# Two-layer graph attention: the last layer norm of each row block is spread over the next sweep and given to GpSimd, and the last sweep is closed by halves

## The reference, cut to what matters

```python
def _L1_gnn_ref(x, W, a, adj_matrix):          # x: 4096 x 256, W: 4 heads x 256 x 64
    xt = jnp.einsum('ni,hio->hno', x, W)
    src = jnp.einsum('hnf,hf->hn', xt, a[:, :out_f])
    dst = jnp.einsum('hnf,hf->hn', xt, a[:, out_f:])
    e = jax.nn.leaky_relu(src[:, :, None] + dst[:, None, :], NEG_SLOPE)
    e = jnp.where((adj_matrix > 0)[None, :, :], e, -jnp.inf)
    attention = jax.nn.softmax(e, axis=2)
    h_prime = jnp.einsum('hij,hjf->hif', attention, xt)
    return h_prime.transpose(1, 0, 2).reshape(n, heads * out_f)

def _layernorm(x, axis=-1, eps=1e-5):
    m = jnp.mean(x, axis=axis, keepdims=True)
    v = jnp.var(x, axis=axis, keepdims=True)
    return (x - m) / jnp.sqrt(v + eps)

x = _layernorm(x + _L0_gnn_ref(x, adj, ...))   # layer 0, 8 heads of 128
x = _layernorm(x + _L1_gnn_ref(x, W, a, adj))  # layer 1, the part looked at here
```

## Time and profile before

| | |
|---|---|
| median of 3 runs | 2784.57 us |
| the profiled execution, own time | 2785.78 us |
| its span | 2783.4 us |
| PE busy | 2680.3 us (96%) |
| DVE busy | 1988.7 us (71%) |
| ACT busy | 2064.6 us (74%) |
| POOL busy | 570.7 us (21%) |
| granted TensorE clock | 0.993 |

### The profile page before, as it was taken

One profiled execution on the slowest core, in us unless ns is written; L12 is line 12 of the kernel. 1 busy time (PEld: TensorE's weight loads), 2 busy tenths in 40 slices (PEclk: granted clock), 3 DMA queues, 4 the chain that ended last, 5 costly groups with the idle time before them and its releaser, 6 DMA issues. The chain is left out here.

```text
span 2783.4 us, 62400 instructions
## 1 busy us (share of the span) xinstructions
PE 2680.3 (96%) x26475; PEld 2323.0 (83%) x26475; DVE 1988.7 (71%) x3200; ACT 2064.6 (74%) x3216; POOL 570.7 (21%) x453
## 2 busy tenths in 40 slices
PE   7889999999999999999999999999999979999997
PEld 3438887888888888888888888888888879999997
DVE  5465679677676776767777676675655779988897
ACT  4447886777777777777777778777754569999996
POOL 0030018232231422323322232230002320000000
PEclk9999999999999999999999999999999999999999
DMA  7985431010110111111111111011115555323330
GB/s 258 395 322 182 141 116 48 22 36 21 42 30 27 37 27 32 33 31 30 34 30 30 26 33 34 26 39 39 38 58 177 189 192 185 114 79 122 103 109 17
DMA packets 193945, 243.70 MB, mean 88 GB/s; under 512 B 14202, under 2 KB 113786, under 8 KB 193660
## 3 DMA queue, kind: packets, MB, share of 16 engines
q1 hardware_dynamic: 193668, 239.72, 26.8%
HBM read 180.49 MB, written 59.18 MB: 86 GB/s over the span
## 5 line engine op out<-in xcount | busy, mean ns | idle before, releaser
L708 PE MATMUL l_ps<-l_arena 128*128 128x258 f16 x16384 | 1835.1, 273 | 8.0 <-DVE l_arena L1214 3.9
L708 PEld LDWEIGHTS l_ps<-l_arena 128*128 128x128 fp8e4 x16384 | 1592.1, 97 | 248.7 <-DVE l_arena L1214 5.5
L923 ACT ACTIVATE l_arena<-l_arena 128x512 fp8e4<-128x512 f32 x2048 | 1281.4, 708 | 89.2 <-PE l_ps L708 89.1
L1213 DVE SCALAR_TENSOR_TENSOR l_arena<-l_arena,l_mask 128x512 uint32<-128x512 uint32 x512 | 469.0, 916 | 405.7 <-ACT l_arena L923 403.0
L817 PE MATMUL l_ps<-l_arena 128*128 128x130 f16 x8192 | 487.8, 221 | 30.0 <-DVE l_arena L1393 15.6
L817 PEld LDWEIGHTS l_ps<-l_arena 128*128 128x128 fp8e4 x8192 | 483.0, 98 | 34.7 <-DVE l_arena L1393 24.7
L1214 DVE TENSOR_TENSOR l_arena<-l_arena,l_mask 128x512 uint32<-128x512 uint32 x512 | 489.9, 957 | 0.0
L1007 ACT ACTIVATE l_arena<-l_arena 128x1024 fp8e4<-128x1024 f32 x432 | 454.7, 1140 | 5.7 <-PE l_ps L817 5.7
L360 POOL TENSOR_TENSOR l_arena<-l_arena 128x516 f32<-128x516 f32 x120 | 156.7, 1306 | 1263.1 <-PE l_ps L708 1171.7
L941 ACT COPY l_arena<-l_ps 128x258 f32<-128x258 f32 x256 | 93.5, 368 | 245.3 <-PE l_ps L708 245.3
L1219 DVE SCALAR_TENSOR_TENSOR l_arena<-l_ps,l_arena 128x258 f32<-128x258 f32 x256 | 117.0, 481 | 147.9 <-ACT l_arena L941 147.9
(11 more groups left out here) (150 smaller groups left out, 1220.6 us busy)
## 6 DMA issues: line engine op xcount, KB each, us to landing
l_arena<-in_adj SPq DMA_DIRECT2D x128, 512.0 KB, 6.9
l_arena<-uv SPq DMA_DIRECT2D x128, 260.0 KB, 5.5
l_wh<-l_arena SPq DMA_DIRECT2D x64, 256.0 KB, 9.3
l_arena<-l_srow SPq DMA_DIRECT2D x64, 256.0 KB, 3.3
l_arena<-l_wh SPq DMA_DIRECT2D x64, 256.0 KB, 4.7
feat<-l_arena SPq DMA_DIRECT2D x64, 256.0 KB, 2.2
l_arena<-feat SPq DMA_DIRECT2D x32, 512.0 KB, 3.7
uv<-l_arena SPq DMA_DIRECT2D x8, 1040.0 KB, 5.2
```

The costliest lines, as they stand in the source:

```text
L708: last = nc.tensor.matmul(sums(t, m), pattern(k, m).bitcast(F8)[:, j, t * P:(t + 1) * P], uv[:, slot(h, order[k]) + j, 2 * m * W1:2 * (m + ...
L923: ins = act.activation(pattern(k, 0).bitcast(F8)[:, j, :], s1b[q][:, :], ACT.Relu, bias=kc[:, h, jt:jt + 1], scale=STEEP, saturate=False)
L1213: dve.scalar_tensor_tensor(c, v, ONE8X4, m, ALU.bitwise_xor, ALU.bitwise_and)
```

## The change

There are four parts.

- **Statistics in two lots.** In g = 4, 8, 12 VectorE takes the statistics of four tiles behind the split of piece 2 and of four behind that of piece 3; only then come the aggregation and the sum with epsilon. The root on ScalarE stands behind the compares of piece 6 (it stood behind those of piece 3), the reciprocal behind the split of piece 6 (it stood behind that of piece 4).
- **Scaling on GpSimd.** The eight instructions `(z - mean) * rstd` of those sweeps leave VectorE. GpSimd, which has no other work in layer 1, does them as eight `tensor_scalar` of 128x256 with two operands per partition, and signals after four and after eight.
- **Halves.** SyncE stores `z` in two halves of 512 KB as they are signalled, then waits for each store and loads that half of the next block. The addition in `divide2` waits for both loads.
- **The last sweep.** In sweep 15 TensorE takes pieces 6 and 7 together and tile by tile: all matmuls of row tile 0, then of tile 1, and so on. VectorE evacuates, divides and takes the statistics of the first four tiles ahead of the second four; ScalarE scales the first four tiles and two of the others, VectorE the last two; three stores follow, of 512, 256 and 256 KB.

The rest (one semaphore fewer for GpSimd's `scale2`, two unused names) moves nothing.

The core of the diff:

```diff
+            for b in range(NB2 - 1):
+                pool.wait_ge(s_rs2, b + 1)
+                for p in range(2):
+                    for u in range(p * HALF, (p + 1) * HALF):
+                        last = nc.gpsimd.tensor_scalar(z[:, u, :], z[:, u, :], mv[:, u, 0:1], rs[:, u:u + 1],
+                                                       ALU.subtract, ALU.mult)
+                    last.then_inc(s_ap, 1)
...
                 if g > 0 and g % H2 == 0:
-                    sp.wait_ge(s_ap, 2 * (g // H2))
-                    sp.dma_start(tiles(out, g // H2 - 1), z[:, :, :]).then_inc(s_o, 16)
-                    sp.wait_ge(s_o, 16 * (g // H2))
-                    sp.dma_start(z[:, :, :], tiles(x1, g // H2)).then_inc(s_zl, 16)
+                    b = g // H2 - 1
+                    for p in range(2):
+                        sp.wait_ge(s_ap, 2 * b + p + 1)
+                        sp.dma_start(tiles(out, b, p * HALF, (p + 1) * HALF), z[:, p * HALF:(p + 1) * HALF, :]
+                                     ).then_inc(s_o[p], 16)
+                    for p in range(2):
+                        sp.wait_ge(s_o[p], 16 * (b + 1))
+                        load_z(b + 1, p)
...
-                for k in range(CPB):
+                for k in range(CPB - 2 if g == G2 - 1 else CPB):
...
+                if g == G2 - 1:
+                    pe.wait_ge(s_bc2, CPB * G2)
...
+                    for t in range(TPB2):
+                        for k in range(CPB - 2, CPB):
+                            for j in range(JC2):
...
+                        if t < TPB2 - 1:
+                            last.then_inc(s_mm2, 1)
+                    last.then_inc(s_pe2, 2)
...
-                    if g > 0 and g % H2 == 0 and k == ahead2 + 1:
+                    if g > 0 and g % H2 == 0 and k == CPB - 2:
                         final_root(g // H2 - 1)
...
-                        if m == 0:
-                            final_stats(g // H2 - 1, range(TPB2))
-                            final_norm(g // H2 - 1)
-                        if m == 2:
-                            final_scale(g // H2 - 1)
-                        if m in (3, 4):
-                            final_apply(g // H2 - 1, range(4 * (m - 3), 4 * (m - 2)), s_ap)
+                        b = g // H2 - 1
+                        if m < 2:
+                            final_stats(b, range(HALF * m, HALF * (m + 1)), g)
+                        if m == 1:
+                            final_norm(range(TPB2), 2 * NT + 3 * b + 2)
+                        if m == 4:
+                            final_scale(range(TPB2), b + 1)
...
-            final_stats(NB2 - 1, range(TPB2))
-            final_norm(NB2 - 1)
-            final_scale(NB2 - 1)
...
-            final_apply(NB2 - 1, range(TPB2 // 2), s_fin[0])
+            evacuate2(G2 - 1, halves[0])
+            divide2(G2 - 1, 0, HALF, 3 * (G2 - 1))
+            final_stats(NB2 - 1, halves[0], G2)
+            final_norm(halves[0], base + 1)
+            evacuate2(G2 - 1, halves[1])
+            final_scale(halves[0], NB2)
+            last_shift(0)
+            divide2(G2 - 1, HALF, TPB2, 3 * G2)
+            final_stats(NB2 - 1, halves[1], G2 + 1)
+            final_norm(halves[1], base + 4)
+            final_scale(halves[1], NB2 + 1)
+            last_shift(1)
+            for u in range(HALF, HALF + 2):
+                last = dve.tensor_scalar(z[:, u, :], z[:, u, :], mv[:, u, 0:1], rs[:, u:u + 1], ALU.subtract, ALU.mult)
+            last.then_inc(s_fin[1], 1)
```

More of the change, by code:

```diff
@@ L202, in network @@
         CW2 = blk2 // 4
+        HALF = TPB2 // 2
         G2, FIRST = H2 * NB2, H2
@@ L630, in _ @@
                         load_uv(g + 2, k)
-            for p in range(2):
+            for p, (first, last) in enumerate(((0, HALF), (HALF, HALF + 2), (HALF + 2, TPB2))):
                 sp.wait_ge(s_fin[p], 1)
-                sp.dma_start(tiles(out, NB2 - 1)[:, p * TPB2 // 2:(p + 1) * TPB2 // 2, :],
-                             z[:, p * TPB2 // 2:(p + 1) * TPB2 // 2, :]).then_inc(s_o, 16)
-            sp.wait_ge(s_o, 16 * (NB2 + 1))
+                sp.dma_start(tiles(out, NB2 - 1, first, last), z[:, first:last, :]).then_inc(s_o[p % 2], 16)
+            sp.wait_ge(s_o[0], 16 * (NB2 + 1))
+            sp.wait_ge(s_o[1], 16 * NB2)
         @block.tensor
@@ L825, in sweep2 @@
                     last.then_inc(s_pe2, 1)
+                if g == G2 - 1:
+                    pe.wait_ge(s_bc2, CPB * G2)
+                    for k in range(CPB - 2, CPB):
+                        pe.wait_ge(s_uv2[q][k], 16 * (g // 2 + 1))
+                    for t in range(TPB2):
+                        for k in range(CPB - 2, CPB):
+                            for j in range(JC2):
+                                jt = order[k] * JC2 + j
+                                for m in range(2):
+                                    at = jt * W4 + m * 2 * V1
+                                    last = nc.tensor.matmul(sums2(t, m),
+                                                            pattern2(k, m).bitcast(F8)[:, j, t * P:(t + 1) * P],
+                                                            uv2[:, q, at:at + 2 * V1], start=False,
+                                                            stop=(k == CPB - 1 and j == JC2 - 1 and m == 1),
+                                                            skip_group_check=True)
+                        if t < TPB2 - 1:
+                            last.then_inc(s_mm2, 1)
+                    last.then_inc(s_pe2, 2)
             pe.wait_ge(s_id, 4)
@@ L1023, in final_root, with last_root, last_apply @@
                 act.activation(rt[:, :], rt[:, :], ACT.Sqrt).then_inc(s_sq, 1)
+            def last_root(p):
+                half = slice(p * HALF, (p + 1) * HALF)
+                act.wait_ge(s_sd, NB2 + p)
+                act.activation(rt[:, half], rt[:, half], ACT.Sqrt).then_inc(s_sq, 1)
+            def last_apply(p, tiles, signal):
+                act.wait_ge(s_n, 2 * NT + 3 * (NB2 + p))
+                for u in tiles:
+                    ins = act.activation(z[:, u, :], z[:, u, :], ACT.Identity, bias=mv[:, u, 1:2], scale=rs[:, u:u + 1])
+                ins.then_inc(signal, 1)
             for n in range(16):
@@ L1111, in _ @@
                 copy_sums2(g, batch)
[L1112 to L1116 removed]
+            last_root(0)
+            last_apply(0, range(HALF), s_fin[0])
+            last_root(1)
+            last_apply(1, range(HALF + 2, TPB2), s_fin[2])
         @block.vector
@@ L1393, in split2, with evacuate2 @@
                 dve.tensor_tensor(v, v, m, ALU.bitwise_and).then_inc(s_bc2, 1)
-            def evacuate2(g):
-                for t in range(TPB2):
+            def evacuate2(g, tiles):
+                for t in tiles:
                     if g == 0 and t == 0:
@@ L1403, in evacuate2, with divide2, final_stats @@
                                              e2[:, t, :], ALU.mult, ALU.add).then_inc(s_ev2, 1)
-            def divide2(g):
+            def divide2(g, first, last, base):
                 h, b = g % H2, g // H2
-                dve.wait_ge(s_ev2, TPB2 * (g + 1))
-                ch = Chain(dve, s_dv2, 3 * g)
-                ch.link(dve.tensor_tensor(vt2, vt2, e2[:, :, V1:2 * V1], ALU.add))
-                ch.link(dve.reciprocal(zr2[:, :], vt2[:, :, D2:V1].rearrange("p t a -> p (t a)")))
-                v = vt2[:, :, 0:D2]
-                ch.link(dve.tensor_tensor(v, v, zr2[:, :].unsqueeze(2).to_broadcast([P, TPB2, D2]), ALU.mult))
-                if h == 0:
-                    dve.wait_ge(s_zl, 16 * (b + 1))
-                part = z[:, :, h * D2:(h + 1) * D2]
-                dve.tensor_tensor(part, part, v, ALU.add).then_inc(s_dz, 1)
-            def final_stats(b, tiles):
-                dve.wait_ge(s_dz, H2 * (b + 1))
+                dve.wait_ge(s_ev2, TPB2 * g + last)
+                ch = Chain(dve, s_dv2, base)
+                part = vt2[:, first:last, :]
+                inverse = zr2[:, first:last]
+                ch.link(dve.tensor_tensor(part, part, e2[:, first:last, V1:2 * V1], ALU.add))
+                ch.link(dve.reciprocal(inverse, part[:, :, D2:V1].rearrange("p t a -> p (t a)")))
+                v = part[:, :, 0:D2]
+                ch.link(dve.tensor_tensor(v, v, inverse.unsqueeze(2).to_broadcast([P, last - first, D2]), ALU.mult))
+                if h == 0:
+                    dve.wait_ge(s_zl, 32 * (b + 1))
+                into = z[:, first:last, h * D2:(h + 1) * D2]
+                dve.tensor_tensor(into, into, v, ALU.add).then_inc(s_dz, 1)
+            def final_stats(b, tiles, ready):
+                dve.wait_ge(s_dz, ready)
                 for u in tiles:
```

71 lines of the change are left out of this document (35 added, 36 removed).

## The result

| | before | changed |
|---|---|---|
| median, 6 runs each | 2784.82 us | 2809.05 us |
| range | 2783.91 to 2788.46 | 2807.52 to 2812.72 |
| span of the profiled execution | 2783.4 us | 2811.0 us |

The ratio is 1.0087, 95% interval 1.0076 to 1.0097: 24.2 us slower. The forecast was 2784.3 in a range of 2776.5 to 2793, that is, no change that could be told, so it was wrong; slower had a chance of 0.26.

The account below looks back on a forecast made before the run. TensorE, busy 96% of the span, was taken as the bound, with only its gaps and the end to win. Three blocks at +2.7 and the last sweep at -3.0 gave -0.3 us: 2784.3 us, range 2776.5 to 2793.

Parts of the forecast that it names:

- Part 1: Norms inside layer 1: two statistics lots and the later root leave about 1.2 us of each norm's 4.2 us loss.
- Part 4: Last sweep: pieces 6 and 7 tile by tile and closing by halves save 3.0 us, between 2.1 and 3.5.
- h: Time one GpSimd scaling holds VectorE up, taken as 0.3 us; three blocks change by 3 x (8h - 1.5).
- Part 2: Scaling on GpSimd: eight alternate with 7.5 us of VectorE work from 2664.8, ending at 2674.7; VectorE up to 2.1 us later.
- Part 3: Half transfers: second half stored by 2678.1, loaded by 2681.8; VectorE's addition waits 3.9 us, all passed to TensorE.
- rival 2: GpSimd's scaling leaves VectorE alone: eight take 3.6 us, `z` is there at 2675.5, total 2772.6; chance 7%.
- the line through the casts: GpSimd one-input casts, 0.253 us at 16 columns and 0.289 at 128, extended to 0.33 at 256: h = 0.1.
- The high end: GpSimd's scaling as dear as a two-input instruction of 256 columns, 0.724 us: h = 0.6.
- the prediction's own rule: From layer 0's overlapping GpSimd and VectorE instructions: h is the GpSimd instruction's length less 0.2 us.
- about -2 us: The forecast's sum if GpSimd's scaling costs the Trainium skill's estimate of 0.22 us for 256 columns.
- Rival 1: GpSimd's scaling is dear, h above 0.55: over 5.6 us slower, 2791.5 at 0.6 and 2796 at 0.8; chance 26%.

Follow-up runs that it names:

- e6: Changed kernel with a product of two SBUF inputs (`z` times `z`) in place of each GpSimd scaling; 2798.11 us, one run.
- e8: Changed kernel with the root behind the compares of piece 5 and the reciprocal behind the split of piece 5, both 6 before; 2810.32 us, 1.0083.
- e9: Changed kernel whose GpSimd scaling keeps the mean per partition but takes a constant for the root; 2808.98 us, one run.
- e12: Changed kernel with root and reciprocal both behind piece 7 instead of piece 6, so GpSimd starts later; 2809.95 us, 1.0088.
- e5: Changed kernel with two constants instead of the two operands per partition in GpSimd's scalings; 2798.54 us, one run.
- e2: Changed kernel with a second buffer for `z` for odd blocks, next block loaded beforehand, scaling still on GpSimd; 2772.21 us, 0.9955 against the kernel before.
- e1: Changed kernel with the eight scalings of sweeps 4, 8, 12 back on VectorE; 2779.82 us, 0.998 against the kernel before.

## Why the prediction was wrong

The path was right (GpSimd's end, store, load, addition, TensorE), and Parts 1 and 4 held. What failed is the size h of Part 2; a smaller part came from the load of a half in Part 3, and the clock behind a gap had no term. The last norm inside the layer, step by step. Times after are put on the clock of before by taking off 21.94 us (2672.04 - 2650.10, both the start of piece 2 of sweep 12).

| step | predicted | measured |
|---|---|---|
| gaps before pieces 3 and 4 (Part 1) | 0.4, 0.75 | 0.33, 0.56 |
| root's wait (Part 1) | none | none |
| reciprocal issued (Part 2) | 2664.8 | 2664.5 |
| eight scalings end (Part 2) | 2674.7 | 2679.7 |
| last scaling to `z` loaded (Part 3) | 7.1 | 8.2 |
| VectorE is ready to add (Part 3) | 2677.9 | 2678.4 |
| its wait (Part 3) | 3.9 | 9.5 |
| 512 matmuls behind the gap longer (no term) | 0 | 2.55 |
| last matmul to end (Part 4) | 11.8 | 11.3 |

**Part 1 held.** The root now starts behind a compare without a wait, where it stood idle 4.86 us:

```profile
2675.77 5.30 ACT L1043 ACTIVATE l_arena<-l_arena 128x1024 fp8e4<-128x1024 f32 x5
2680.97 0.20 ACT L1059 ACTIVATE l_arena<-l_arena 128x8 f32<-128x8 f32 x1
```

**Part 2 failed**, in the step "GpSimd's eight alternate with them: the last ends at 2664.8 + 7.5 + 8h = 2674.7". Two things in it were wrong. The size: the instruction takes 1.21 us without splits beside it, not 0.45 (rival 2) or 0.5 (h = 0.3 and the 0.2); the upper bound, 0.724 for a two-input instruction of the same size, was no bound at all, since the operation with two constants takes 1.06 and a plain product in e6 0.61. One input is not the cheap case here: the line through the casts did not hold for this operation. The high end was mis-stepped too: 0.724 less 0.2 is 0.52, not 0.6. And the form of the sharing: I took from layer 0's pairs that the engines take turns, so that h comes back on VectorE. That is so for two-input instructions (e6). With an operand per partition VectorE keeps its 1.22, and GpSimd waits, mostly for its pauses (e8, e9, e12). VectorE lost 0.5 us, GpSimd's end 5.0.

Of the two, the size made the loss. By the prediction's own rule 1.21 us give h = 1.0, and the last scaling would end at 2664.8 + 7.5 + 8.1 = 2680.4, 0.7 past the measured 2679.7. Three norms at that h cost 3 x (8.1 - 1.5) = 19.8, and with Part 4 that is 2784.6 + 19.8 - 3.0 = 2801.4; three times the 1.1 of the load and the 6.9 of the clock (both below) make it 2811.6, against 2809.05 measured. The same working for e6 (h = 0.41, 6.0 us behind its gaps) gives 11.6 us over the kernel before, where its one run has 10.8. That the wrong form of sharing came so near in GpSimd's end is luck: in e8 and e12 the start moved and the end hardly did, which no rule of taking turns gives.

A row of the kernel before already pointed at the other form. Rival 2 used the cast L381 that took 1.25 us instead of 0.25, but not what ran beside it, a split instruction that kept its 1.21:

```profile
2267.98 1.25 POOL L381 CAST l_arena<-l_arena 128x16 f16<-128x16 f32 x1
```

```profile
2267.91 1.21 DVE L1392 SCALAR_TENSOR_TENSOR l_arena<-l_arena,l_mask 128x1024 uint32<-128x1024 uint32 x1
```

In that pair GpSimd alone was held up.

The Trainium skill's rule ("SBUF — State Buffer", Who interferes with whom), that such a pair excludes each other for a whole instruction, agrees with e6 (1.63 for a split's instruction, 1.59 for GpSimd's). The same section of the Trainium skill says "Issue order, not op shape, decides who blocks." That does not agree with the runs: e5, e6 and e9 start GpSimd's work at the same place in the code and differ in the instruction alone, and who is held up changes; and in e8 seven instructions of VectorE that started later were done before the one of 9.00 us. The measurement decides.

The estimate of 0.22 us from the Trainium skill, "GPSIMD Engine Reference", 3.1, is off by a factor of 5 against 1.06 to 1.21. The prediction's "about -2 us" by it took h = 0.22; by its own rule, length less 0.2, h is 0.02 and the sum -7.0.

**Part 3** took that end over, one to one as it says: 5.0 more from the scaling, 1.1 more from the transfers, 0.5 less since VectorE was itself that late, 3.9 + 5.0 + 1.1 - 0.5 = 9.5. The halves on the queue and the half transfers:

```profile
2696.84 5.20 SPq L632 DMA_DIRECT2D out<-l_arena  x2
2702.08 3.15 SPq L501 DMA_DIRECT2D l_arena<-x  x2
```

```profile
out<-l_arena SPq DMA_DIRECT2D x2, 512.0 KB, 3.1
l_arena<-x SPq DMA_DIRECT2D x2, 512.0 KB, 4.8
```

The store of a half takes 3.1 to 3.2, about as forecast (3.3). The load was to take 3.7, since I took off it what the store saves; it takes 4.8. It is issued at 2704.86, 2.8 us behind the first, with row and values for later sweeps 0.5 and 1.0 behind it, and the DMA engines are over 90% busy until it lands. How much of the 1.1 each of these costs was not separated:

```profile
2703.40:2705.00 1.60, 0.07 (x2) 0.00 (x0) 0.00 (x0) 1.60 (x3) 0.00 (x0) 1.00 0.99 211
2705.00:2707.00 2.00, 0.00 (x0) 0.00 (x0) 0.00 (x0) 2.00 (x3) 0.00 (x0) 0.60 0.93 269
2707.00:2709.70 2.70, 0.00 (x0) 0.00 (x0) 0.00 (x0) 2.70 (x3) 0.00 (x0) 0.50 0.93 313
```

(Windows: start:end, length, busy time of PE, PEld, DVE, ACT and POOL, granted clock, DMA share, GB/s.)

**A term was missing.** TensorE's granted clock falls in the gap (1.00, 0.60, 0.50 in the windows above) and is low behind it. More windows, same columns:

```profile
2713.50:2716.50 3.00, 3.00 (x29) 3.00 (x30) 3.00 (x4) 0.00 (x0) 0.00 (x0) 0.50 0.84 324
2716.50:2719.50 3.00, 3.00 (x34) 3.00 (x33) 2.12 (x2) 0.00 (x0) 0.00 (x0) 0.57 0.04 12
2719.50:2722.50 3.00, 3.00 (x55) 3.00 (x53) 2.52 (x3) 2.52 (x3) 0.00 (x0) 1.00 0.00 0
```

At 0.50, that is 1.2 GHz, 29 matmuls start in 3 us; at 1.00, in the last window, 55. This costs 2.54, 1.79 and 2.55 us behind the three gaps, 6.9 in sum, over a quarter of the loss of 24.2.

For this norm: 1.2 + 9.5 + 2.55 = 13.3, against 13.45 from the stretch (105.10 less three sweeps of 30.55) and 5.1 as forecast.

**Part 4 held**: 3.5 against 3.0, and no gap before the last 128 matmuls. From the last matmul to the last scaling it is 8.4 us where it was 10.7, and from there to the end 2.9 where it was 4.1.

**The rivals.** Rival 1 named the right place and sign, "an instruction of 0.75 us or more", at 26%. Its price was too low: it stopped at h = 0.8 (2796), where 1.0 was due, and it had neither the slower load nor the clock. Rival 2's premise, VectorE left alone, came nearly true (0.5 us), but its conclusion was the opposite of what happened. I took it that if VectorE is not held, GpSimd isn't either. Who is not held and who is was one question in the forecast, and it is two.

## What to carry to other kernels

A step moved to an idle engine is free only while nobody waits for its end. Follow its end through every buffer back to the bounding engine before moving it, and give it a second buffer first: e2 turned a loss of 24 us into a gain of 12 without making GpSimd a bit quicker. Where no row shows an instruction in its very form, a row of the same size in another form is no upper bound, and a row alone does not tell who is held up beside a busy VectorE; read both engines' rows where they overlap. Add to any forecast gap of TensorE of 5 us or more what its clock costs behind it, here 1.3 to 2.7 us.

## What the runs showed of the hardware

- GpSimd, 128x256 f32 without splits beside it: product 0.61 us (e6), two constants 1.06 (e5), one operand per partition 1.14 (e9), two 1.21.
- A `tensor_scalar` on GpSimd with an operand per partition makes way for VectorE's splits: up to 9.00 us for one (e8), the splits at 1.22. With a product both suffer, 1.59 and 1.63 (e6). With constants it lies between: 1.36 in the median on GpSimd, up to 1.42 for a split's instruction (e5).
- Evacuations, whose one input is in PSUM, let it go on: the instruction at 2696.80 takes 1.21 us, with four evacuations beside it from 2697.28.
- A gap of 2.42 us before piece 2 of a sweep cost no clock (e1: the next 512 matmuls took 30.20 us). Behind gaps of 4.92 to 13.00 us they took 31.51 to 32.94, and the longer gap was not the dearer one: 4.92 was followed by 31.65 and 5.57 by 32.52 (e6), 12.70 by 31.73 (e8), 10.01 by 32.75 (the changed kernel).
